# First wide attention: part of the softmax sums added on VectorE ahead of the sums' product

## What is computed

```python
q = (xn @ w_q).reshape(b, n, HEADS, DIM_HEAD).transpose(0, 2, 1, 3)
...
q = _l2norm(q) * q_scale
k = _l2norm(k) * k_scale
sim = jnp.einsum('bhid,bhjd->bhij', q, k) * ATTN_SCALE
...
sim = jnp.where(causal_mask[None, None], neg, sim)
attn = jax.nn.softmax(sim, axis=-1)
out = jnp.einsum('bhij,bhjd->bhid', attn, v)
out = out.transpose(0, 2, 1, 3).reshape(b, n, HEADS * DIM_HEAD)
return out @ w_out
```

## Time and profile before

| | us |
|---|---|
| median of 3 runs | 2560.18 (2559.87 to 2560.31) |
| profiled execution, its own time | 2552.11 |
| its span, first to last instruction | 2550.4 |
| PE busy in the span | 2348.4 (92%) |
| DVE, ACT, POOL busy | 1604.4, 1470.3, 1595.8 |
| first wide attention | the first 790 of the span |

### The profile page before, as it was taken

The page is one execution under the profiler, slowest core; times in us unless marked ns, Lnnn a source line. Parts: engine busy times, 40 slices in busy tenths (PEclk is TensorE's granted clock), DMA queues, the critical chain, the costliest instruction groups (busy, mean ns, idle before and its releaser), DMA issues. The chain is left out here.

```text
span 2550.4 us, 61619 instructions
## 1 busy us (share of the span) xinstructions
PE 2348.4 (92%) x23721; PEld 1820.9 (71%) x23721; DVE 1604.4 (63%) x4234; ACT 1470.3 (58%) x3038; POOL 1595.8 (63%) x2569
## 2 busy tenths in 40 slices
PE   6999999999998699988999999999999968788897
PEld 5888888888886366656777788777877757455555
DVE  5666666666664277774455477777777622577776
ACT  5666666666664377764444466666656523466665
POOL 6888888888884444443333277777777722566664
PEclk8999999999999789999999999999999989899999
DMA  8930000000000100001000000000000045000000
GB/s 295 328 129 2 2 2 2 2 2 2 2 2 1 40 7 2 2 2 33 1 1 1 3 4 4 6 6 6 4 6 6 4 145 172 15 10 8 8 4 34
DMA packets 22915, 82.91 MB, mean 33 GB/s; under 512 B 3969, under 2 KB 10882, under 8 KB 21602
## 3 DMA queue, kind: packets, MB, share of 16 engines
q1 hardware_dynamic: 19474, 71.76, 8.8%
q0 software_dynamic: 3152, 7.21, 0.9%
HBM read 71.76 MB, written 46.79 MB: 46 GB/s over the span
## 5 line engine op out<-in xcount | busy, mean ns | idle before, releaser
L978 POOL TENSOR_TENSOR XR<-XR,T 128x256 f32<-128x256 f32 x504 | 369.0, 732 | 36.9 <-DVE T L858 7.3
L722 ACT ACTIVATE P<-ps 128x384 f32<-128x384 f32 (+1 forms) x512 | 250.7, 542 | 179.9 <-PE ps L2691 178.4
L2691 PE MATMUL ps<-P,V 128*64 128x256 f32 (+3 forms) x4096 | 332.0, 345 | 9.2 <-DVE O L1482 7.9
L1466 DVE TENSOR_REDUCE bm<-ps 128x3 f32<-128x384 f32 x512 | 260.0, 549 | 105.5 <-PE ps L2691 104.6
L2691 PEld LDWEIGHTS ps<-P,V 128*64 128x64 f32 (+1 forms) x4096 | 185.5, 123 | 131.0 <-issue 44.7
L1401 ACT ACTIVATE P<-ps 128x768 f32<-128x768 f32 x256 | 207.7, 811 | 99.6 <-PE ps L2691 99.1
L889 DVE TENSOR_REDUCE sm<-ps 128x2 f32<-128x512 f32 (+1 forms) x256 | 129.9, 549 | 187.6 <-PE ps L2691 187.6
L1567 POOL TENSOR_SCALAR_AFFINE_SELECT P<-P 128x512 f32<-128x512 f32 x256 | 162.6, 635 | 119.1 <-ACT P L1401 116.3
L991 POOL TENSOR_TENSOR PS<-P 128x256 f32<-128x256 f32 x256 | 181.5, 734 | 70.7 <-ACT P L722 70.4
L2691 PE MATMUL ps<-mk,identb 128*128 128x256 bf16 (+1 forms) x1024 | 202.6, 292 | 14.4 <-DVE bm L1466 11.3
L1012 POOL TENSOR_TENSOR ss<-ss,nhalf 128x16 f32<-128x16 f32 x64 | 187.7, 2933 | 5.3
(11 more groups left out here) (310 smaller groups left out, 6853.2 us busy)
## 6 DMA issues: line engine op xcount, KB each, us to landing
rows_i<-in_zero SPq DMA_DIRECT2D x16, 1208.0 KB, 31.9
rows_o<-in_zero SPq DMA_DIRECT2D x16, 1208.0 KB, 81.8
w<-in_m_w SPq DMA_DIRECT2D x23, 578.0 KB, 4.1
zt<-rows_i SPq DMA_DIRECT2D x23, 128.0 KB, 3.2
rows_o<-yo POOLq DMA_DIRECT2D x23, 128.0 KB, 3.9
stg<-in_t_w SPq DMA_DIRECT2D x11, 256.0 KB, 2.8
XR<-in_x SPq DMA_DIRECT2D x4, 512.0 KB, 8.9
out<-XR SPq DMA_DIRECT2D x8, 256.0 KB, 2.0
```

Source lines behind the costliest of these rows:

```text
L722: e.activation(self.P[at % 6][:, :], K.ps.ap("st", s, g, h)[:, 0:self.w], ACT.Exp, bias=0.0, scale=1.0 if kind == 0 else 0.125).then_inc(K ...
L978: p = po.e.tensor_tensor(x, x, self.T[g % 2][:, par, pr], ALU.add)
L1466: e.tensor_reduce(bm[:, h, :], K.ps.ap("mx", s, g, h)[:, 0:384].rearrange("p (a c) -> p a c", c=128), X, ALU.max, negate=True).then_inc(K. ...
L2691: return self.te.matmul(o, l, r, start=start, stop=True, skip_group_check=True)
```

## The change

In kind 0 there is a new tile PS (two of [128, 4, 128]) and a semaphore `halved`. One tick after the exponentials of two heads, DVE adds for each of the two heads the columns 128 to 255 of P (key tile 0, query tile 1) and 256 to 383 (key tile 1, query tile 1) into PS and raises `halved`. PE waits for all four heads' additions and then makes the sums' product of 128 columns of P (query tile 0) and 128 columns of PS (query tile 1). V's product is as before.

```diff
@@ class Wide, __init__
         if kind == 0:
             self.raw = [sb(f"raw{s}_{i}", [128, 512], F32) for i in range(6)]
+            self.PS = [sb(f"PS{s}_{i}", [128, 4, 128], F32) for i in range(2)]
+            self.halved = K.sem(f"halved{s}")
@@ pe_pv
         if kind == 0:
-            for kt, q, c, w in self.blocks():
+            pe.wait_ge(self.halved, 4 * g + 4)
+            for qt in range(2):
                 for h in range(4):
-                    p = K.acc(sm[32 * h:32 * h + 32, q:q + w], self.one[:, 0:32], P[h][:, c:c + w], start=kt == 0)
+                    p = K.acc(sm[32 * h:32 * h + 32, 128 * qt:128 * qt + 128], self.one[:, 0:32],
+                              self.PS[g % 2][:, h, :] if qt else P[h][:, 0:128], start=qt == 0)
             p.then_inc(K.ps.full_of("sm", s, g), 1)
@@ dve_unit
         if kind == 0 and k == self.tk["mx"] - 1:
             self.dve_null(dv, b, u)
+        n = self.part("st", k - 1)
+        if kind == 0 and n is not None:
+            if g >= 2:
+                dv.wait_ge(*K.ps.filled("sm", s, g - 2))
+            for h in (2 * n, 2 * n + 1):
+                P = self.P[(4 * g + h) % 6]
+                dv.wait_ge(*K.ps.read("st", s, g, h))
+                e.tensor_tensor(self.PS[g % 2][:, h, :], P[:, 128:256], P[:, 256:384], ALU.add).then_inc(self.halved, 1)
         n = self.part("mx", k)
```

## The result

| | us |
|---|---|
| after, median of 4 runs | 2623.01 (2620.08 to 2628.03) |
| before, median of 4 runs beside them | 2560.02 (2558.47 to 2560.31) |
| ratio | 1.0249 (95%: 1.0231 to 1.0267) |
| profiled execution of after: its own time, span | 2624.95, 2623.3 |

The change costs 63 us. Between the two profiled executions it is 73 us, because that of before lies 8 us under its median and that of after 2 us over.

A forecast was written before the change was run, and what follows sets the result against it. TensorE was taken to set the time, so added waits lengthen the run: 14 groups of four units at 4.15 us plus 5.3 for the last eight make 63 us, giving 2623 us (range 2600 to 2645).

The forecast's parts named there:

- The place of the pair, and PE's wait for it: Additions of heads 2 and 3 stand behind QL and ahead of KL on DVE; PE waits for them before the sums' product.
- rival that a short pass is no cheaper: Sums' product on PE: passes over 128 columns save nothing in their place, 14 us more, 2637 us; chance 0.04.
- Unit 2, +2.90: The unit of four with layer norm steps ahead of the pair: +2.10 undisturbed, and +0.80 for one held addition.
- the second addition is held for one of the two scalings: In unit 2 DVE's second addition is held for one of POOL's two scalings of 1.02 us each: +0.80 us.
- undisturbed pair: Rival: POOL and DVE miss each other in unit 2, which costs +2.10; 56 us in all, 2616 us; chance 0.33.
- Unit 3, -0.10: With unit 2 at 2.90, unit 3 is bound by PE's own pace and its pair, 0.10 us under before.
- 91% should keep it: PE, idle about 1.1 of 12.7 us, stays busy enough at 91% to keep its granted clock of 1.00.
- clock rival: PE's idle pieces lower its clock; a tenth of the stage at 1.2 GHz adds 50 to 70 us, 2680; chance 0.05.
- The last eight units, +5.3: Units 56 on, with the next stage's layer norm steps: waits of 8.9 us, less 1.8, with 8 x 0.22 gained.
- The additions of heads 0 and 1 at nothing: Just ahead of the second maxima DVE idles 0.88 us in three units of four; the pair's 0.50 fits, costing nothing.
- KL's start + 0.60: PE can start the sums when KL started before, plus 0.50 us for the pair and 0.10 for the way to PE.
- faster: Rival: the additions are in time, PE never waits, 14 us are gained, 2546 us; chance 0.04.

The follow-up runs named there:

- e1: The kernel before with only the shorter sums' product (128 and 128 columns), no additions, key tile 0 left out for query tile 1: 2556.92 against 2559.95 us.
- e6: The changed kernel with two small DVE reductions ahead of unit 2's pair of additions, so that it starts after POOL's scaling has begun: 2672.52 us.
- e5: The changed kernel with extra PE products into unused columns ahead of unit 2's wait for the additions: 2615.73 us.
- e4: The changed kernel with the layer norm steps of unit 2's tick put behind KL on DVE, not ahead of the pair: 2629.93 us.
- e8: The kernel before with only DVE's layer norm steps moved: unit 2's behind KL, the second z behind the first maxima: 2548.55 us beside 2556.69.
- e2: The kernel before with the four DVE additions a unit alone; PE neither waits for them nor reads PS: 2572.27 against 2559.95 us.
- e3: The changed kernel with heads 2 and 3 added right behind the second maxima's small steps, ahead of squares' sum, T and QL: 2577.14 against 2562.58 us.
- e7: The changed kernel with that early pair, layer norm steps behind KL, and second z behind first maxima and squares' sum: 2559.43 us beside 2562.58.

## Why the prediction was right, and where it was not

The time was forecast at 2623 and is 2623.0, but two terms of its sum were wrong and cancelled. That the two agree within 1 us is luck, as the terms below show.

- **The place of the pair, and PE's wait for it**: right. All 64 units wait. In units 0 and 1 the waits are 0.74 and 0.77 us (about 0.9 expected), in unit 2 2.17 (2.3 to 4.2 expected). Costs +0.60 and +0.58 against +0.66 and +0.69. The way from the pair to PE was taken as 0.10 us; the pair ends at 597.42 and PE starts at 597.48, 0.06.
- **The sums' product**: right, 0.58 us (0.57 in the sum, 0.79 in before), a saving of 0.21 a unit and not 0.22. The rival that a short pass is no cheaper falls by e1.
- **The additions**: right in size. The median record is 284 ns (293 taken), a pair 0.46 us (0.50). The first addition of heads 0 and 1 is held in units 0 and 2, beside POOL's additions into XR: medians of 0.49 and 0.47 us, within DVE's idle time there.
- **Unit 2, +2.90**: the step that failed is "the second addition is held for one of the two scalings". It wasn't held, and the unit cost +2.02, close to the rival's +2.10. That rival (undisturbed pair) was right on this term. The second addition is 0.05 us ahead of the scaling in after, and e6, with the pair 0.36 us later, shows the price of being behind it: both scalings, 1.65 us, not one. The mechanism was real, its outcome here a matter of hundredths of a microsecond that no row of before could settle, and its size was taken too small.
- **Unit 3, -0.10**: the step that failed is "91% should keep it", said of the clock. Without the fall the unit costs +0.06 (12.30 in three groups), between the +0.16 of the undisturbed case and the -0.10 of the held one; with it, +1.42. I compared PE's mean share over whole stages, and what counted was one wait of 2.17 us between busy stretches. The clock rival had a chance of 0.05 and a price of 50 to 70 us; it did happen, for 3.4 us at a time, and its price is 13.6 us in the steady part (e5, e4). Its places, just behind the longest wait, were not in the prediction.
- **Together**: 0.88 us too much in unit 2, 1.20 too little in unit 3 and 0.17 too much in units 0 and 1, so 4.30 against 4.15. The sum was made for the profiled execution and said 63 us there; by its spans it is 73: 2.0 us more in the 13 groups, 0.5 ahead of them, 2.0 in the last eight units and 4.9 behind the stage. The medians differ by 63 and not by 73 because before's profiled execution lies 8 us under its median and after's 2 us over; the sum did not foresee that. Had the pair been held as well, by both scalings, the time would have been near that of e6, 2672 less some 5 for its reductions (an estimate, 14 x 0.36), well outside the range of 2600 to 2645.
- **The last eight units, +5.3**: measured +7.3. Of this 3.3 us is unit 57 (16.09 against 12.79 us). The windows of after show 3.6 us in which PE is busy for 1.2, and then 6.8 us at the lower clock; without these the term is +4.0.

```profile
775.00:778.60 3.60, 1.21 (x26) 0.70 (x20) 3.56 (x11) 0.67 (x3) 3.18 (x10) 0.99 0.00 0
778.60:782.00 3.40, 3.40 (x17) 3.40 (x18) 0.95 (x4) 1.16 (x3) 3.32 (x2) 0.50 0.00 0
782.00:785.40 3.40, 3.40 (x26) 2.78 (x27) 0.00 (x0) 1.24 (x3) 3.24 (x6) 0.50 0.00 0
```

- **"PE sets the time there, and every us that it is kept waiting goes onto the end"**: true of units 0, 1 and 2, false of unit 3. In before's windows by unit PE is busy all of 399.10 to 410.25 and of 422.51 to 433.66, and 11.97 of 12.26 us in unit 3 between them: it already waits there, behind the z that waits for POOL. e1 gives back there 0.21 of the 0.63 us that it gains in the other three, and e8 gains 0.56 us there (0.29 are that idle time; where the rest came from was not looked into). The sum did not suffer, since unit 3 was costed by its own chain.
- **The additions of heads 0 and 1 at nothing**: right in unit 2 (0.29 us of idle time is left). Four additions together are not free: e2 prices them at 12 us without any wait for them, through KL. In the sum this was covered by the term "KL's start + 0.60", since PE waits for the pair ahead of KL anyway; the rival "faster" would have been 2546 only if they were free in every place, and e3 and e7 show 2577 and 2559 instead, with the pair in the place that this rival named.
- **The budget of waits** closes: 69.0 us of waits for PS, 13.6 and 3.3 us of lower clock, less 64 x 0.21 = 13.4 us for the product, make 72.5; the spans differ by 72.9. Waits of before that went away and the 4.9 us behind the stage, where single profiled executions differ by as much, are not in that sum, so the agreement within 0.4 is partly luck.

Three of the 13 groups (unit 3 at units 15, 27 and 47) keep the full clock behind the same wait, of 2.16 to 2.17 us in all 13. The traces show what separates them: the falls of after begin a multiple of 51.20 us apart (for example at 597.65 and 700.05), and the wait moves against that row of times from group to group. The ten waits that a fall follows end between 0.92 us ahead of such a time and 0.13 us behind it; the three others end 0.18 to 0.43 us behind one. In e4 it is 1.08 ahead to 0.05 behind, against 0.39 to 0.50 behind. So whether such a wait costs the clock went by its place in time and not by its length. This is read from two traces; no run moved the wait on purpose.

Open: that the fall in unit 57 has the same cause as those in the steady part was not tried.

## What to carry to other kernels

Cost an instruction that is added to an in-order engine by its place in the queue: by what stands ahead of it and what behind it must be ready for whom, since an engine with a third of its time free made these four additions cost 12 us with nobody waiting for them, and the whole change 63 us with TensorE waiting. When a wait of TensorE is new, price the clock after it too: a wait of about 2 us cost 1.4 us more in ten groups of 13, and work put into it took that away. Before saving matmul columns, see whether TensorE is the late one in every unit of the pattern; here the order of VectorE's steps in one unit of four was worth 8 us, and without it the shorter product gave 3 us of the 14 that were counted on.

## What the runs showed of the hardware

**The clock falls after a short wait.** A wait of 2.17 us between stretches in which PE is busy is followed by 3.4 us at granted clock 0.5 in ten cases of 13 (after), one of 2.20 us in nine of 13 (e4), one of 4.16 us by 6.8 us in all 13 (e6). With waits of at most 0.8 us (e5, steady part) it never fell. Which of the 2.2 us waits lost the clock went by when they ended, as told above. The Trainium skill (TensorE: Matmul & The Clock Gate, "Why this matters for your kernels") warns of idle gaps between bursts of products that are longer than the 2.2 us seen here; by it the clock would have held in after and in e4. It fell in ten and in nine cases of 13, and the measurement decides.

**A shared port turns on less than two tenths of a microsecond.** Two additions of 128x128 take 0.46 us when the second starts 0.05 us ahead of POOL's scaling (after), and 2.11 us when the first starts 0.13 us behind it (e6). In the first case it is POOL that pays, with 0.09 us. Not every instruction of POOL holds them: additions that start inside its power (2.94 us, L1024) take 0.28 us each in units 0, 1 and 3 of after.
